# A recurrence's input product moved from ScalarE to VectorE, and a TensorE wait changed, in an eight-core transformer block

## What is computed

```python
ah = jnp.tanh(a)
bx = b * xn                                  # the product that the change moves
y  = scan(u_t = ah * u_(t-1) + bx_t)         # along the tokens, for each of 1024 channels
branch1 = y @ w_out.T + b_out

def layer(x):                                # twice, with its own weights
    h = shift_token(x)
    q, k, v = split(h @ wqkv)                # 8 heads of 64
    q, k = rotary_xpos(l2norm(q)*qs, l2norm(k)*ks)
    x = x + local_attention(q, k, v) @ wo    # window 512
    h = layernorm(shift_token(x))
    a, g = split(h @ w1 + b1)                # 2 x 2730
    return x + (a * gelu(g)) @ w2 + b2
out = x + branch1 + layer(layer(xn))
```

## Time and profile before

| | |
|---|---|
| time, three runs | 2938.35 us median (2933.51, 2938.35, 3089.05) |
| the profiled execution | 2930.28 us; span of its slowest core 2928.7 us, of all cores 2920.1 to 2928.7 us |
| TensorE matmuls busy | 2065.5 us (71%) |
| VectorE busy | 1082.5 us (37%), 1833 instructions |
| ScalarE busy | 623.3 us (21%), 1034 instructions, 69 of them table loads |
| mean granted TensorE clock | 0.753 of full speed on the slowest core |

### The profile page before, as it was taken

The page is one execution under the profiler, slowest core; times in us unless marked ns, Lnnn a source line. Parts: engine busy times, 40 slices in busy tenths (PEclk is TensorE's granted clock), DMA queues, the critical chain, the costliest instruction groups (busy, mean ns, idle before and its releaser), DMA issues.

```text
span 2928.7 us, 27800 instructions; the slowest of 8 cores (2920.1 to 2928.7 us)
## 1 busy us (share of the span) xinstructions
PE 2065.5 (71%) x9488; PEld 931.8 (32%) x9488; DVE 1082.5 (37%) x1833; ACT 623.3 (21%) x1034; POOL 35.4 (1%) x50
## 2 busy tenths in 40 slices
PE   1277576799776674999225777758996767659994
PEld 1122232344322341444112223323442333314442
DVE  4705445311135445111373344453111444462113
ACT  1233331210023322110023233302100323312100
POOL 0000000000010000000000000000000000000000
PEclk9986556799885556999557855568998755569996
DMA  5249930122359800222332300001213200002223
GB/s 86 79 51 101 110 42 29 39 77 58 44 68 110 97 12 25 72 65 72 115 108 37 43 1 1 1 29 52 73 58 41 36 1 1 1 29 69 66 60 123
DMA packets 123856, 159.74 MB, mean 55 GB/s; under 512 B 48211, under 2 KB 90708, under 8 KB 122500
## 3 DMA queue, kind: packets, MB, share of 16 engines
q0 software_dynamic: 30624, 52.42, 15.7%
q1 hardware_dynamic: 93092, 105.53, 12.7%
HBM read 201.95 MB, written 44.03 MB: 84 GB/s over the span
## 4 chain that ended last, share of the span: by engine, by line
PE 59%; DVE 22%; ACT 5%; issue 5%; DMA 4%; SPq 2%; DVEq 1%; ACTq 0%; POOLq 0%
PE psA L1634 11%; PE psA L1192 8%; DVE UN L333 8%; PE psA L1613 5%; PE psA L1617 5%; PE psB L1613 5%; PE psB L1617 5%; DVE Bb L333 4%; DVE attnT L333 4%; PE psB L971 4%; PE psA L882 3%; PE psB L1231 3%; PE psA L1344 2%; DMA out<-UN 2%; ACT L333 2%
## 5 line engine op out<-in xcount | busy, mean ns | idle before, releaser
L333 ACT ACT_TABLE_LOAD x69 | 88.5, 1283 | 1097.7 <-PE psA L1192 368.2
L1613 PE MATMUL psB<-stg,WS 128*128 128x512 bf16 x704 | 277.3, 394 | 49.2 <-ACT stg L333 49.2
L1617 PE MATMUL psB<-stg,WS 128*128 128x512 bf16 x704 | 277.7, 394 | 0.0
L1613 PE MATMUL psA<-stg,WS 128*128 128x512 bf16 (+1 forms) x704 | 269.8, 383 | 0.0
L1617 PE MATMUL psA<-stg,WS 128*128 128x512 bf16 (+1 forms) x704 | 269.2, 382 | 0.0
L1634 PE MATMUL psA<-Bb,WS 128*128 128x512 bf16 x1024 | 232.8, 387 | 11.1 <-DVE UN L333 11.1
L1192 PE MATMUL psA<-Bb 64*128 64x128 bf16 (+3 forms) x432 | 179.3, 415 | 34.8 <-ACT probs L333 30.0
L333 ACT ACTIVATE probs<-psA 128x640 bf16<-128x640 f32 (+5 forms) x264 | 171.4, 649 | 95.5 <-PE psA L1192 68.7
L1231 PE MATMUL psB<-attnT,Bb 128*64 128x128 bf16 x960 | 79.1, 311 | 144.1 <-DVE attnT L333 144.1
L882 PE MATMUL psA<-stg,WS 128*128 128x512 bf16 x512 | 138.2, 432 | 34.7 <-DVE stg L333 20.1
L333 DVE TENSOR_TENSOR UN<-UN 128x1024 bf16<-128x1024 bf16 (+1 forms) x48 | 41.8, 870 | 314.2 <-ACT UN L333 277.1
(11 more groups left out here) (118 smaller groups left out, 2485.8 us busy)
## 6 DMA issues: line engine op xcount, KB each, us to landing
WS<-wpre SPq DMA_DIRECT2D x184, 256.0 KB, 2.9
wpre<-w1p POOLq DMA_DIRECT2D x8, 2730.0 KB, 71.0
WS<-wpre SPq DMA_DIRECT2D x96, 224.0 KB
UN<-x SPq DMA_DIRECT2D x32, 512.0 KB, 4.5
WS<-wqkv POOLq DMA_DIRECT2D x24, 512.0 KB, 6.6
wpre<-w2p POOLq DMA_DIRECT2D x4, 2730.0 KB, 146.7
out<-UN SPq DMA_DIRECT2D x16, 512.0 KB, 5.3
Bb<-c_tabhi SPq DMA_DIRECT2D x8, 512.0 KB
```

The lines of the kernel that those rows point to most:

```text
L333: ins = f(*a, **kw)
L1613: t.matmul(rA[0:ln, tc * 512:(tc + 1) * 512], wu[:, kt * ln:(kt + 1) * ln], B.stg[kt][:, tc * 512:(tc + 1) * 512], start=(kt == 0), stop=( ...
L1617: ins = t.matmul(rG[0:ln, tc * 512:(tc + 1) * 512], wu[:, 1024 + kt * ln:1024 + (kt + 1) * ln], B.stg[kt][:, tc * 512:(tc + 1) * 512], sta ...
```

## The change

In `phase_scan` the product with `bcol` is done on VectorE, in its own queue directly in front of each scan, into a single buffer; ScalarE's eight multiplications and the waits between the two engines go away. In `phase_qkv` the wait in front of chunks 3 to 10 is for ScalarE's eviction of the chunk three before it, where it was for the n2 matmul of that chunk. For chunk 11 both are the same event.

```diff
@@ phase_p0, emit_tp
                 u_evac[tb] = B.ev(B.sV, ins)
-                if tb == 7:
-                    B.u_evac_last = u_evac[7]
@@ phase_scan
         ycast_ev = [None] * NG
-        bx_ev = [None] * NG
-        BXS = [PKS, PKS - 1024]
-
-        vb0 = B.sV.n
-        per_g = 3 if h == 0 else 2
-
-        @blk.scalar
-        def _(sc):
-            sc = B.S
-            B.w(sc, "scalar", B.u_evac_last)
-            for g in range(NG):
-                if g >= 2:
-                    B.wf(sc, "scalar", (B.sV, vb0 + per_g * (g - 2) + 1))
-                bx_ev[g] = B.ev(B.sS, sc.activation(
-                    B.un(BXS[g % 2], H), B.u[g][:, 1:H + 1], AF.Identity,
-                    scale=B.bcol[:, g:g + 1]))
-
         for g in range(NG):
             @blk.vector
             def _(v):
 
                 v = B.V
-                B.w(v, "vector", bx_ev[g])
+                e = B.ev(B.sV, v.tensor_scalar_mul(
+                    B.un(PKS, H), B.u[g][:, 1:H + 1], B.bcol[:, g:g + 1]))
+                B.w(v, "vector", e)
                 init = 0.0 if h == 0 else B.carry[:, g:g + 1]
                 d0 = B.ah8[:, g:g + 1].broadcast_to([128, H])
                 e = B.ev(B.sV, v.tensor_tensor_scan(
-                    B.Bb[g][:, 0:H], d0, B.un(BXS[g % 2], H), init,
-                    ALU.mult, ALU.add))
+                    B.Bb[g][:, 0:H], d0, B.un(PKS, H), init, ALU.mult, ALU.add))
@@ phase_qkv, emit_chunk_mm
                 if c >= 3:
-                    B.wf(t, "tensor", cons_ev[c - 3])
+                    B.wf(t, "tensor", qevac_pred[c - 3] if c - 3 < 8
+                         else vevac_pred[c - 11])
```

## The result

The changed kernel takes 2947.62 us (median of 11 runs) against 2938.35 us. The ratio of their undisturbed runs is 1.0038, with a 95% interval of 1.0028 to 1.0049: 11.1 us slower (8.2 to 14.4). In a comparison that asks for 2% this is no change; it is a real loss all the same, and its interval excludes zero.

What follows compares the result with a forecast made beforehand. No engine fills the span; in the scan stage VectorE is the path. Sixteen steps of 0.78 us add 12.5 us, the wait nothing; put on 2935.9 this gives 2948 us, range 2936 to 2964.

Steps and rivals of the forecast that it cites:

- The bound of the stage: Scan stage: VectorE runs back to back, period 3.52 and 3.32 us; ScalarE's 1.15 us multiplications are hidden, removing them gains nothing.
- The price of the product: New VectorE multiplication in the scan stage: 749 ns, from 221 fixed plus 1024 x 0.516; bounds 681 and 1284 ns.
- The gaps: Around each product: two gaps of 0.10 us replace one of 0.17; each step grows 0.78 us, sixteen by 12.5.
- Nothing behind it hides or gives back: Behind the scans: projection, column loads, wqkv loads and parking evictions all move by 6.2 us in each half.
- The wait: TensorE before QKV chunks 3 to 10: both events already past, no stall to win; cost and gain nothing.
- rival 1: Scan stage: the multiplication runs at the slow rate, 1284 ns; +21.0 us, 2957; chance 0.12.
- rival 2: Scan stage: VectorE pays a flush behind each extra instruction, 0.48 us each; sum 20.2 us, 2956; chance 0.03.
- rival 3: Between last scan and scaling of qs: delay swallowed, stretch shrinks by 6 us in each half; 2936; chance 0.05.
- rival 4: Scan stage: VectorE's new instruction locks POOL out of descriptor generation, wqkv loads late; 12 us more, 2960; chance 0.01.
- rival 5: QKV chunks: later start leaves TensorE at the 1.2 GHz level; slower by over 2%, all chunks 3072; chance 0.02.
- faster by over 2%: Whole kernel: an outcome with no case behind it, 0.01 kept for what the prediction hadn't seen.
- The level: Whole kernel: forecast put on 2935.9, the mean of the two lower runs shown; 2948 us, 0.4% above before; chance 0.77.

Runs made afterwards that it cites:

- early columns: Kernel before, SyncE issuing layer 0's eleven column loads at the scan stage's start: 0.9958; also with product on VectorE: 0.9997; with ScalarE's scaled casts in one block: 0.9914.
- the doubled product: Changed kernel with the product computed twice on VectorE, the first time into an unused buffer: ratio 1.0067 (1.0037 to 1.0098).

## Why the prediction was right, step by step

**The bound of the stage.** "VectorE is the path, ScalarE is hidden" held from both sides: taking the product away altogether changed nothing that the times show (1.0005; one pause of 0.2 us in the stage), taking the cast and the gap away from VectorE gave 10.3 us.

**The price of the product.** It was put together from two rows, 221 ns fixed and 0.516 ns an element, as 749 ns, and 753 were measured. The bounds, 681 and 1284, were never close to deciding. The Trainium skill's formula, quoted in the prediction from "VectorE: DVE Perf Modes" (section on the trn2 errata), gave an estimate of 594 ns, so the row was the better guide.

**The gaps.** Two of 0.10 for one of 0.17 was right. The step was put at 0.78 us and came out at 0.79 to 0.80; a sum of 12.5 us was forecast and 12.48 measured in the stages. One thing I passed over: in the first half before, one of the seven periods was 3.72 and not 3.52 us long, on every core, by a pause that the changed kernel doesn't have. That is why this half grew by 6.14 us and not by 6.3.

**Nothing behind it hides or gives back.** The chain's links came in the same order, shifted. In the first half the stretch to the first eviction kept its length (44.97 and 45.04 us). In the second it was 0.9 us shorter, and the stretch from the last scan's start to the scaling of qs, which I had said would stay within 47 to 50 us, was 44.5 us on core 6 (47.1 as a mean of all; 48.3 in the first half). The bounds came from two cores in one half, and were too narrow for eight: in the second half of the kernel before the eight cores already have 46.7 to 50.0. The kernels with untouched column loads have 43.5 to 45.4 us there, so nothing is read into the 0.9.

**The wait.** Nothing was forecast, and nothing is seen. The prediction named the 32 matmuls of the earlier trace rows chunks 8 and 9; they are chunks 9 and 10, since chunk 8 goes to `psB`. The pair has a wait of the changed kind between its halves all the same, so the reading holds for them. TensorE's chunks in the changed kernel:

```profile
178.61 5.62 PE L865 MATMUL psA<-stg,WS 128*128 128x512 bf16 x16 [7.09 <-DMA WS<-wqkv]
...
197.92 3.63 PE L865 MATMUL psB<-stg,WS 128*128 128x512 bf16 x16
...
242.35 7.07 PE L865 MATMUL psA<-stg,WS 128*128 128x512 bf16 x32
```

3.63 for one and 7.07 for two, as in the earlier trace rows; the first, behind idle time, takes 5.62 us here and took 6.47.

**The rivals.** The slow rate (rival 1) is excluded by the 753 ns row. The flush (rival 2) would have been a gap of 0.48 us; the gap is 0.10. Swallowed (rival 3) was to show as a stretch from last scan to qs that is 6 us shorter in each half; it went from 48.2 to 48.3 us and from 48.2 to 47.1, and the kernels with early columns and the doubled product speak against it too. The lock of POOL (rival 4) could not act, since POOL's first issue is still behind the scans:

```profile
168.65 0.92 POOL L379 DMA_DIRECT2D WS<-wqkv  x1 [150.65 <-PE psA L700]
```

The clock (rival 5): the mean granted clock of the cores was 0.751 to 0.755, and 0.753 to 0.755 before. In the projection it was 1.00 in the first half of both kernels and 0.93 in the second of both, and in the four QKV phases 0.88, 0.88, 0.88, 0.89 before and 0.89, 0.87, 0.87, 0.89 after; the phases add up to 303.7 and 302.3 us. So the later start cost no clock. (The prediction's 12 matmuls in the first 4 us were counted from 134.00; from the projection's start at 133.33 they are 10.)

The chances of the forecast and the five rivals add up to 1.00, and the 0.01 kept for "faster by over 2%" comes on top; the 0.97 for "within 2%" leaves it room, the list of the rivals doesn't.

**The level.** 2948 was the mean of the two lower runs shown, plus 12.5. It landed on 2947.62. The starting point, 2935.9, was 0.7 us under the median of the undisturbed runs of before (2936.6 of eight), and the effect in the runs was 11.1 and not 12.5: two small errors that cancel in part. That the level was met to half a microsecond is luck; the sum that gave the difference is not. The interval of 8.2 to 14.4 holds the 12.5; whether the missing 1.4 us is real stays open.

## What to carry to other kernels

An operation that is hidden on one engine costs its full duration on the other, and whatever it adds in gaps (0.75 and 0.04 us here), when it is moved into the chain which sets the stage; ask first which engine's chain has no idle time in that stage, and price the new instruction as the fixed part of one row plus the slope of another (749 ns against 753 in the one case tried here). When a factor must be applied to a linear recurrence, put it into the cast that is made anyway. Where many activations of one function are issued, issue them from one program block, and let small loads go out in a stretch in which the DMA queues are nearly idle (their busy share was 0.01 and less from 92 to 133 us before), not behind the work that frees the stage.

## What I had not expected of the hardware

- A table load of 1.28 us comes with each program block that holds an activation, even if the function stays the same: 8 in a half with eight blocks, 1 with one block, and one in front of each of the eight parking evictions, which have blocks of their own. It made ScalarE's period 2.57 us where the cast takes 1.15.
- Multiplying by the column of scalars costs 0.06 us in a VectorE cast of 1024 elements (754 against 694 ns), and the product takes 0.07 us more than the clamp with a constant (753 against 681, the clamp on 8 partitions). ScalarE's simultaneous reads and writes don't lengthen a scan: 2.29 and 2.35 us in each kernel, on each core.
- Eleven tiny loads, the largest 10.5 KB, cost the path 6.3 and 6.6 us in the two halves: half of it by their own landing, 2.4 us because the large load beside them landed later, and the rest in a chunk at a lower granted clock.
